# A drain instruction between TensorE's last product of a chunk and the news of it

## The reference, cut to what matters

```python
q_att = jnp.einsum('nhd,rhde->rnhe', q, relation_att)
v_msg = jnp.einsum('nhd,rhde->rnhe', v, relation_msg)
aw_q_edge = q_att[etype, col_idx]
msg_edge = v_msg[etype, row_idx]
attn_score = jnp.sum(aw_q_edge * k[row_idx], axis=-1)
score = attn_score * (relation_pri[etype] / SQRT_DK)
m = jax.ops.segment_max(score, col_idx, num_segments=n)
ex = jnp.exp(score - m[col_idx])
denom = jax.ops.segment_sum(ex, col_idx, num_segments=n)
alpha = ex / denom[col_idx]
agg = jax.ops.segment_sum(alpha[..., None] * msg_edge, col_idx, num_segments=n)
```

## Time and profile before

| | |
|---|---|
| time, median of 3 (lowest to highest) | 2216.26 us (2209.56 to 2218.08) |
| span of the profiled execution | 2447.7 us |
| mean granted TensorE clock over it | 0.931 |
| TensorE products busy | 1985.2 us, 81% |
| VectorE busy | 1665.7 us, 68% |
| ScalarE busy | 1461.7 us, 60% |
| GpSimd busy | 1179.5 us, 48% |
| edge loop, first to last `expand` product | 562 to 1973 us |

### The profile page before, as it was taken

How to read it: one execution, slowest core, us unless ns; L and a number is a source line. 1 busy time by engine, 2 the same in 40 slices (tenths; PEclk the granted TensorE clock), 3 DMA queues, 4 the chain that set the end, 5 groups by cost and what they waited for, 6 DMA issues and landing times.

```text
span 2447.7 us, 37644 instructions
## 1 busy us (share of the span) xinstructions
PE 1985.2 (81%) x10414; PEld 1482.6 (61%) x10414; DVE 1665.7 (68%) x4120; ACT 1461.7 (60%) x4981; POOL 1179.5 (48%) x1207
## 2 busy tenths in 40 slices
PE   6999997995788888888888888888888865803999
PEld 5865554554566676666776667666676644602666
DVE  8957765553688787778878878778887783626111
ACT  5845554562477777667767777776777663610222
POOL 0033334335566666555666666666566504651221
PEclk9999999997899999899999999999999897955999
DMA  5868879997788888787888878888888728831120
GB/s 181 302 227 321 325 312 273 337 377 254 219 275 271 261 290 265 240 256 254 267 270 258 268 254 278 261 267 268 264 280 274 227 71 265 281 141 35 35 63 28
DMA packets 271666, 587.06 MB, mean 240 GB/s; under 512 B 45058, under 2 KB 185672, under 8 KB 264802
## 3 DMA queue, kind: packets, MB, share of 16 engines
q0 software_dynamic: 93936, 387.70, 47.3%
q1 hardware_dynamic: 177522, 196.94, 25.2%
HBM read 407.93 MB, written 176.99 MB: 239 GB/s over the span
## 4 chain that ended last, share of the span: by engine, by line
PE 49%; DVE 20%; issue 11%; ACT 8%; another core or an unknown queue 8%; DVEq 2%; DMA 2%; SPq 0%; POOL 0%; POOLq 0%; ACTq 0%
PE bank L962 9%; PE bank L781 7%; PE bank L946 6%; ACT arena L1329 5%; PE bank L1119 4%; PE bank L1130 4%; PE bank L760 4%; PE bank L927 3%; DVE arena L1933 3%; DVE arena L2026 2%; PE bank L629 2%; PE bank L842 2%; DVE arena L1990 2%; PE bank L918 2%
## 5 line engine op out<-in xcount | busy, mean ns | idle before, releaser
L2317 POOL DMA_INDIRECT arena<-table,arena x880 | 863.3, 981 | 549.6 <-issue 218.7
L1329 ACT ACTIVATE arena<-arena 128x64 f32<-128x64 f32 x3448 | 841.0, 341 | 0.0
L962 PE MATMUL bank<-arena 128*128 128x260 f32 x1760 | 470.2, 405 | 114.2 <-issue 78.8
L962 PEld LDWEIGHTS bank<-arena 128*128 128x128 f32 x1760 | 328.2, 197 | 216.3 <-issue 148.9
L1933 DVE TENSOR_TENSOR arena<-bank,arena 128x512 f32<-128x512 f32 x440 | 301.9, 687 | 199.2 <-remote 150.2
L946 PE MATMUL bank<-arena 128*128 128x256 bf16 x2640 | 346.4, 280 | 26.6 <-issue 26.5
L946 PEld LDWEIGHTS bank<-arena 128*128 128x128 bf16 x2640 | 265.6, 101 | 94.7 <-issue 32.4
L1943 DVE TENSOR_REDUCE arena<-arena 128x16 f32<-128x1024 f32 x220 | 267.7, 1217 | 17.2
L781 PE MATMUL bank<-arena 64*128 64x512 f32 x832 | 209.9, 620 | 20.7 <-DVE arena L1675 15.2
L2026 DVE TENSOR_TENSOR arena<-arena,bank 128x260 f32 x440 | 185.0, 420 | 43.9 <-remote 23.4
L1213 ACT COPY arena<-bank 128x512 f32<-128x512 f32 x260 | 148.9, 595 | 86.7 <-PE bank L781 79.2
(11 more groups left out here) (316 smaller groups left out, 3084.0 us busy)
## 6 DMA issues: line engine op xcount, KB each, us to landing
arena<-q_parts SPq DMA_DIRECT2D x440, 192.0 KB
arena<-chunk_rel SPq DMA_DIRECT2D x220, 128.0 KB
arena<-table,arena POOLq DMA_INDIRECT x880
node_rows<-arena SPq DMA_DIRECT2D x24, 512.0 KB, 7.2
xl_and_sum<-arena SPq DMA_DIRECT2D x8, 1536.0 KB
arena<-in_x SPq DMA_DIRECT2D x12, 512.0 KB, 7.8
xn<-arena SPq DMA_DIRECT2D x12, 512.0 KB, 8.7
xT<-arena SPq DMA_DIRECT2D x12, 512.0 KB, 8.2
```

The source lines that it names most:

```text
L962: ins = TE.matmul(bank[b][:, 0:AW], lhsT=so[p % 2][:, c % 2, j, :], rhs=values_of(c, j), start=j == 0, stop=j == HALF - 1)
L1329: ins = A.activation(seg, seg, ACT.Copy, scale=rows[:, C + h:C + h + 1])
L2317: G.indirect_dma_start(rows_of_pair(p, i % 2 * HALF + j), None, d_tab_rows[0:N * R, :], bass.IndirectOffsetOnAxis(ap=idxE[:, g, j, c:c + 1 ...
```

## The change

In `expand`, the increment of `full[b]` no longer hangs on the sixth product of a chunk. A drain instruction follows this product on TensorE's queue, and the increment hangs on the drain. It is the whole change:

```diff
                     for s in range(3):
                         ins = TE.matmul(bank[b][:, j * C:(j + 1) * C], lhsT=oh[p % 2][:, (c % 2 * HALF + j) * P:(c % 2 * HALF + j + 1) * P],
                                         rhs=q3r[p % NQ3][:, c % 2, s, :], start=s == 0, stop=s == 2)
-                ins.then_inc(full[b], 1)
+                TE.drain().then_inc(full[b], 1)
 
         def scatter(p):
             TE.wait_ge(targets_made, p + 1)
```

## The result

The changed kernel takes 2260.89 us (median of 4 runs, 2256.43 to 2265.46), the kernel before in the same comparison 2213.01 us: ratio 1.0213, 95% interval 1.0190 to 1.0236. It is slower by 48 us. A second comparison gave 2263.54 against 2211.77 us, ratio 1.0231 (1.0211 to 1.0251), slower by 52 us. The forecast was +94 us, 2310, with a range of 2260 to 2380; the measured time lies at its very lower edge.

The account below looks back on a forecast made before the run. The loop was taken as a pipeline with several engines late in turn, TensorE most often. Of 141 us of holes 92 pass, plus 2 for late news: 94 on 2216 gives 2310 us; range 2260 to 2380, 8 in 10 within 2245 to 2400.

Parts of the forecast that it names:

- The hole: TensorE's queue behind each drain in the edge loop: 0.32 us lost a drain, 440 drains, 141 us.
- tail: Last product before a drain: 0.273 us to its end, successor normally starts after 0.111; 0.162 us lost.
- notice: TensorE's notice of the end and new start after a drain: 0.05 us, from a wait on VectorE.
- weight load: First weight load behind a drain, no longer hidden under a product: 0.11 us.
- The share that passes: Part of the loop's 141 us of holes that reaches the end: between 0.48 and 1, taken 0.65, 92 us.
- The late news: VectorE's `product` hears of the expanded queries 0.05 us later, 91 waits, 5 us at most; 2 counted.
- Holes vanish in the slack: Rival: TensorE's 235 us idle in the loop absorbs the holes, or drains are cheap; 2216 to 2227 us, chance 0.10.
- A dear drain: Rival: 0.57 us a drain in the loop, 0.9 passing, TensorE becomes the bound; 226 us, 2442, chance 0.13.
- The clock: Rival: 440 more pauses lower TensorE's clock in the loop, at most 169 us; 2445 us, chance 0.05.
- Faster: Rival: drain's increment reaches VectorE's `product` 0.08 us sooner at 91 waits; 7 us gained, 2209, chance 0.04.
- Does not do what it says: Rival: the drain returns at once, news comes early; 2216 to 2227 or 2209 us, no chance of its own.
- Waits ahead of `scatter` shorter: Sign: TensorE's waits before `scatter` in the loop shrink by what the holes took of the slack.

Follow-up runs that it names:

- second comparison: The changed kernel timed once more against the kernel before: 2263.54 against 2211.77 us, ratio 1.0231.
- with the increment at the product: Against the kernel before: increment stays at the sixth product, a drain without increment behind it (440 drains); 2268.13 us, ratio 1.0245, where before took 2213.63.
- first comparison: Here the kernel before, run again unchanged for a second profile against itself: 2454.86 us, ratio 1.0002, where before took 2455.06.

## Why the prediction was wrong, point by point

**The hole: right in sum, its parts less so.** Forecast 0.32 us as 0.162 tail, 0.05 notice and 0.11 weight load. Measured 0.24 us behind most drains and 0.39 us behind those that a wait instruction follows, in sum 130 us against 141. In the short kind a drain ends 0.294 us after the last product's start and the next product starts 0.059 or 0.208 us later. Notice and weight load together, which I had at 0.16 us, cost 0.08, and the wait instruction behind the drain, which ran ahead before and so cost nothing, was not in my list; the two misses nearly cancel, by luck. By the rule of the Trainium skill, PSUM — Partial Sum Buffer, section Engine vs sequencer instructions, a drain waits until the engine is idle; the trace agrees, with 0.294 us, 0.021 after the product's shown end, which is modelled.

**The share that passes: wrong, and with it the size.** This is the step that failed: 0.65 was taken, between 0.48 and 1, and 0.37 to 0.40 came (48 to 52 of 130 us; 0.38 for the second drains alone), below even my lower end. That end was the share of `expand` during which TensorE is on the chain, read from the long kind. The same reading of the short kind's trace gives 6.4% of 1237 us = 79 us of the 293 us of stream: 0.27. In the changed kernel it is 10.7% of 1278 us = 137 us: 0.47. The price of holes that grow from nothing to full size should lie between the share before and the share after, and the measured one does. So the kind of reading was right, and my step up from the lower end too, but it began at the wrong end. The reading gives bounds and no value: that the middle of the two is just 0.37 is luck, since in other short traces with a drain behind every chunk the share of `expand` is higher at nearly the same price, 12.1% of 1284 us (0.53) in the second comparison and 16.8% (0.74) with the increment at the product.

That a trace 231 us over the plain runs might be of another kind, I wrote down as unknown and carried its shares over all the same. In it, over half of the semaphore updates are missing (18,593 recorded, 40,898 in the short kind's trace of the same kernel), so what it names as the end of a wait rests on fewer than half of them. I also argued that with less slack in the plain loop more would pass. The slack was smaller there, 172 us of interruptions against 361 in a long trace, and still less passed: the sum of the idle time did not decide.

**The late news: right, and small.** From the sixth product's start to `product` 0.43 us in the changed kernel's trace, 0.41 before: 0.02 instead of 0.05 us. With the news early again, nothing comes back (+55 and, in the long kind, +159 and +172).

**The rivals.** *Holes vanish in the slack*: partly so, some 80 of 130 us, far more than I gave it, but not to within 0.5%. *A dear drain*: not in the short kind. *The clock*: not in the short kind, 0.98 to 0.99; in the long kind it fell from 0.94 to 0.91. *Faster*: no. *Does not do what it says*: no, the holes stand in the trace.

**The signs I named.** Twelve products about 1.8 us: 1.74. Hole behind the second drain: there. Waits ahead of `scatter` shorter: 18.9 and 14.7 us down to 1.4 and 5.1, and all interruptions there by 51 us, more than a third of what the holes add. Loop +94: +46. Only the last is off. My sign of an error, waits ahead of `scatter` shrinking by nearly as much as the holes add, came true only in part: 51 of 130 us there, 85 in the whole loop.

**What the forecast would have been worth in the long kind.** There the same change costs +160 us, ratio 1.058, above the +141 us of my sum with every hole passing and near the upper edge of my range. The one trace that I had would not have told it: in a quarter of the places a drain there ends 0.9 us or more after the last product's start, and the clock falls.

## What to carry to other kernels

A drain behind bf16 products of 256 columns in a running stream made a hole of 0.24 us here, and 0.15 more where a wait instruction followed; leave the increment on the product, which tells 0.02 us earlier and holds up nothing. Of small holes only a part reaches the end, 0.37 to 0.40 here; waits that another engine ends eat the rest, and the share of that place on the chain of waits, 0.27 before and 0.47 to 0.74 after, only bounds that part. And before a sum is made from a trace, compare its span with the plain runs: when they differ by a tenth, as here, the waits, the chain and the clock in it are those of another kind of execution, even where an instruction's duration at the same clock is the same.

## What the runs showed of the hardware that was not expected

- The same kernel takes either about 2212 us or about 2455 us, by the comparison and its chip, 11% apart. At 2.4 GHz a product takes as long in both: TensorE's stream in the loop, counted with the distances at this clock, sums to 1056 to 1057 us. What differs is the interruptions, 172 us in the short kind's loop and 361 in the long (first comparison). Of these 189 us some 46 are slower products, since the long kind's loop ran 166 us at 1.2 GHz and the short one's 55; there a product of `expand` starts 0.213 us after the one before it instead of 0.111. The rest are waits, 77 us of them ahead of `scatter`.
- In the long kind TensorE's increments are recorded late. By the trace's records of semaphores, an increment at a product comes 0.014 us after the product's shown end in the short kind, at all 440 of L962. In the unchanged kernel of the long kind (first comparison) 393 of the 440 have a record before the next product of their bank ends, and it is 0.9 us late in the median; the other 47 have none. Many records are missing there (18,625 updates recorded against 40,898 in the short kind's trace of this kernel). VectorE's wait for expanded queries shows it as waits that nothing recorded ends, in the unchanged kernel of the long kind:

```profile
DVE arena L1933 <- remote: 172.6, 69, 16.7
```

- There a drain also ends late: 0.294 us after the last product's start in the median, as in the short kind, but 0.9 us or more in a quarter of the 440 cases, and 4.8 us or more in 1%. Late increments and late drains fit products that really end later than the trace's modelled ends. VectorE's starts fit it too: of 41 additions ahead of which it stood idle and whose increment is recorded over 0.2 us late, 27 began within 0.2 us after the record. It remains argued, since no record shows a product's true end. What makes them late, and why the second drain of a pair costs 151 to 177 us there and the first only 14 to 22, stays open; that the clock falls with the second and not with the first is the one difference seen.
- In the short kind, taking 77% of the bytes of the loop's gathers away left the time within 4 us, although the mean busy share of the DMA engines in the loop was 0.90 (0.54 without them).
